# A graph network on one core: how the two attention layers end, where their biases are added, and 16-bit step tables

## What is computed

```
h = relu(layernorm(x)); for i in 0..2: h = in_norm * segment_sum((h * out_norm)[src], dst) @ W[i] + b[i]; relu but for the last
x1 = x + h
h = relu(layernorm(x1))
h1 = relu(gat_conv(h, W1, att1) + b1)
out = x1 + gat_conv(h1, W2, att2) + b2
gat_conv: h = x @ W; softmax over each node's incoming edges and itself of leaky_relu(a_src[src] + a_dst[dst]); weighted sum of h[src]
```

## Time and profile before

| | |
|---|---|
| median of 3 runs | 6783.42 us (6779.98 to 6793.79) |
| span of the profiled execution | 5649.0 us |
| difference between the two, outside the span | 1134.4 us |
| convolution 2, first to last gather | 2259.7 to 3237.3 us |
| attention 0, first to last gather | 3314.8 to 4361.8 us |
| attention 1, first to last gather | 4478.0 to 5527.6 us |
| `rs` of attention 1 there | 5563.0 us |

### The profile page before, as it was taken

How to read it: one execution, slowest core, us unless ns; L and a number is a source line. 1 busy time by engine, 2 the same in 40 slices (tenths; PEclk the granted TensorE clock), 3 DMA queues, 4 the chain that set the end, 5 groups by cost and what they waited for, 6 DMA issues and landing times.

```text
span 5649.0 us, 84292 instructions
## 1 busy us (share of the span) xinstructions
PE 4218.4 (75%) x14997; PEld 2470.4 (44%) x14997; DVE 3705.7 (66%) x12168; ACT 2101.0 (37%) x7038; POOL 4159.4 (74%) x4290
## 2 busy tenths in 40 slices
PE   8677777777777778677777777777777677777772
PEld 7433333343333335333333355555554455555551
DVE  7555555555555554555555568777777677777777
ACT  4000000020000003000000088888887688888881
POOL 8677777777777777777777747777776677777776
PEclk7777677787777668777777778878888888888886
DMA  2443333333333333433333354444444344444444
GB/s 94 117 111 106 106 105 106 105 108 106 106 105 105 105 106 100 131 105 105 106 106 106 106 167 110 110 110 110 110 111 125 99 110 110 110 110 110 110 112 151
DMA packets 309459, 625.61 MB, mean 111 GB/s; under 512 B 85044, under 2 KB 180264, under 8 KB 308937
## 3 DMA queue, kind: packets, MB, share of 16 engines
q0 software_dynamic: 192928, 530.18, 33.3%
q1 hardware_dynamic: 109656, 88.65, 5.0%
q10 hardware_dynamic: 6384, 1.39, 0.1%
HBM read 573.37 MB, written 47.33 MB: 110 GB/s over the span
## 4 chain that ended last, share of the span: by engine, by line
PE 40%; POOL 20%; DMA 14%; issue 11%; DVE 10%; ACT 5%; POOLq 0%; DVEq 0%; SPq 0%; ACTq 0%
PE main L1071 20%; POOL ring L667 13%; PE main L1174 11%; DMA ring<-conv_tab,csrc 9%; DMA ring<-attn_tab,sidx 5%; POOL ring L679 5%; DVE acc L1365 3%; PE main L990 3%; POOL ring L699 2%; PE pso L1094 2%; ACT ring L912 2%; DVE ring L1226 1%; ACT oh L890 1%; DVE ad L1584 1%; PE pso L982 1%
## 5 line engine op out<-in xcount | busy, mean ns | idle before, releaser
L667 POOL DMA_INDIRECT ring<-conv_tab,csrc x2346 | 2222.6, 947 | 749.2 <-issue 590.4
L1071 PE MATMUL main<-ring,oh 128*128 x4992 | 2207.0, 565 | 758.2 <-DVE acc L1365 325.1
L1365 DVE TENSOR_TENSOR acc<-acc,main 128x264 f32 (+2 forms) x4160 | 1761.8, 424 | 1254.2 <-PE main L1071 1157.6
L679 POOL DMA_INDIRECT ring<-attn_tab,sidx x1664 | 1590.8, 956 | 604.5 <-issue 361.7
L1071 PEld LDWEIGHTS main<-ring,oh 128*128 128x128 f32 x4992 | 1092.0, 259 | 1869.7 <-issue 1801.3
L1174 PE MATMUL main<-ring,oh 128*128 128x264 f32 x3328 | 1246.2, 491 | 120.6 <-ACT ring L912 69.2
L912 ACT ACTIVATE ring<-ring 128x64 f32<-128x64 f32 x3328 | 910.9, 343 | 0.0
L1357 DVE TENSOR_SCALAR oh<-iota,dloc 128x128 f32<-128x128 f32 x2505 | 814.8, 325 | 91.9 <-issue 79.6
L1174 PEld LDWEIGHTS main<-ring,oh 128*128 128x128 f32 x3328 | 619.3, 229 | 290.3 <-DVE ring L1690 222.8
L890 ACT ACTIVATE oh<-iota,dloc 128x128 f32<-128x128 f32 x1664 | 528.9, 394 | 3.4 <-DMA attn_tab<-oh 3.4
L1690 DVE TENSOR_TENSOR ring<-ring 128x128 f32<-128x128 f32 x1664 | 463.1, 284 | 0.0
(11 more groups left out here) (212 smaller groups left out, 2993.3 us busy)
## 6 DMA issues: line engine op xcount, KB each, us to landing
ring<-conv_tab,csrc POOLq DMA_INDIRECT x2346, 2.7
ring<-attn_tab,sidx POOLq DMA_INDIRECT x1664
ring<-attn_tab SPq DMA_DIRECT2D x14, 896.0 KB, 8.5
conv_tab<-oh SPq DMA_DIRECT2D x12, 896.0 KB, 4.0
flag_room<-start_rows SPq DMA_DIRECT2D x416, 8.0 KB
flag_room<-end_rows SPq DMA_DIRECT2D x416, 8.0 KB
x_tab<-acc SPq DMA_DIRECT2D x7, 896.0 KB
oh<-x_tab SPq DMA_DIRECT2D x7, 896.0 KB
```

The source lines that it names most:

```text
L667: pool.indirect_dma_start(ring3[:, c % U, 0:C], None, conv_tab[k], bass.IndirectOffsetOnAxis(ap=csrc[:, c:c + 1], axis=0)).then_inc(gather ...
L679: pool.indirect_dma_start(ring3[:, j, 0:TW], None, attn_tab[l], bass.IndirectOffsetOnAxis(ap=sidx[:, i * GB * G + j:i * GB * G + j + 1], a ...
L1071: nc.tensor.matmul(main[s % 4][:, 0:width], oh[:, (s % OHR) * P:(s % OHR + 1) * P], ring[:, bass.ds(slots[s % 8], width)], start=True, sto ...
L1365: nc.vector.tensor_tensor(a, a, main[k][:, 0:width], ALU.add).then_inc(added, 1)
```

## The change

- **Own rows by three engines.** Of each block's 7 tiles, DVE weights the first 4 and POOL the last 3 in attention 0; in attention 1 DVE weights 2, ACT 2 (four instructions of 64 columns a tile) and POOL 3.
- **Cuts.** The first block is done as 2 and 5 tiles, the last as 5 and 2.
- **b1** is added and rectified by ACT at the turned copies, where a feature is a partition: two instructions of 128 columns from `pso` to `aT` in place of one copy. PE turns the tiles from `acc` itself. L1521 and L862 are gone.
- **b2** is subtracted from the stored x1 (whose sign is turned, so that it is added at the end): by POOL on tiles 0 to 41, each once ACT has rectified it, and by DVE on tiles 42 to 48 in one instruction after the last `take_tv` of attention 0. SP's stores of x1 wait for that and stand one block later. L1521 is gone from the end of attention 1 too.
- **The last block of the result** is stored in two pieces, as its parts are done.
- **The step table** holds 16-bit values. The number of loads and of values in each is the same.
- Two loads move: b2 comes with the weights before convolution 1, and b1 a second time, one value a partition.

The diff, cut (the removed lines of `rectify_last` and `normalise` stand in the kernel above as well):

```diff
-        step_words = dram("step_words", (4, SX), I32)
+        step_words = dram("step_words", (4, SX), U16)
...
+        b1T = sb("b1T", [P, 2])
...
-        step_tab = flag_room[H * G:H * G + 4, 0:SX].bitcast(I32)
+        step_tab = flag_room[H * G:H * G + 4, 0:SX // 2].bitcast(U16)
...
+        x1_last_biased = summed
+        POOL_X1 = NT - TB
...
+        def cuts(i):
+            a, b = i * TB, (i + 1) * TB
+            return ((a, a + LAST), (a + LAST, b)) if i == 0 else pieces(i)
+        def own_share(l, i):
+            a, b = i * TB, (i + 1) * TB
+            first, mid = (a + 4, a + 4) if l == 0 else (a + 2, a + 4)
+            return first, mid, b
...
-                    load_bias(b1.rearrange("(o c) -> o c", o=1))
+                    load_bias(b2.rearrange("(o c) -> o c", o=1))
+                    with nc.allow_non_contiguous_dma(reason="one bias value a partition"):
+                        sp.dma_start(b1T[:, :], b1.rearrange("(b p) -> p b", p=P)).then_inc(bias_in, 16)
...
+                def store_x1(i):
+                    if (i + 1) * TB <= POOL_X1:
+                        sp.wait_ge(x1_biased, (i + 1) * TB)
+                    else:
+                        sp.wait_ge(x1_last_biased, NT + 1)
+                    sp.dma_start(rows_of(x1_tab, i, C), acc3[:, i * TB:(i + 1) * TB, 0:C]).then_inc(stored, 16)
                 for i in range(0, NI):
                     store_stage(attn_tab[l], TW, HOPS + l, i)
-                    if l == 0:
-                        sp.wait_ge(mid_ready, i * TB + TB)
-                        sp.dma_start(rows_of(x1_tab, i, C), acc3[:, i * TB:(i + 1) * TB, 0:C]).then_inc(stored, 16)
-                if l:
-                    sp.wait_ge(mid_ready, (l + 1) * NT)
-                    load_bias(b2.rearrange("(o c) -> o c", o=1))
+                    if l == 0 and i:
+                        store_x1(i - 1)
+                if l == 0:
+                    store_x1(NI - 1)
...
-            for q in range(NI - XB, NI):
+            for q in range(NI - XB, NI - 1):
                 store_result(q)
+            a, b = pieces(NI - 1)[0]
+            sp.wait_ge(mid_ready, 2 * NT + b)
+            sp.dma_start(out[a * P:b * P, :].rearrange("(t p) c -> p t c", p=P), acc3[:, a:b, 0:C]).then_inc(stored, 16)
+            sp.wait_ge(mid_ready, 3 * NT)
+            sp.dma_start(out[b * P:NFULL * P, :].rearrange("(t p) c -> p t c", p=P), acc3[:, b:NFULL, 0:C]
+                         ).then_inc(stored, 16)
             sp.dma_start(out[NFULL * P:N, :], acc3[0:NREST, NFULL, 0:C]).then_inc(stored, 16)
-            sp.wait_ge(stored, 16 * (2 * NI + 1))
+            sp.wait_ge(stored, 16 * (2 * NI + 2))
...
+            pool.wait_ge(bias_in, 48)
+            for t in range(POOL_X1):
+                pool.wait_ge(nb_ready, (HOPS - 1) * NT + t + 1)
+                pool.nop(nofuse=True)
+                nc.gpsimd.tensor_tensor(acc[:, t * AW:t * AW + C], acc[:, t * AW:t * AW + C], bias[:, :], ALU.subtract
+                                        ).then_inc(x1_biased, 1)
             for l in range(LAYERS):
                 gather_attn(l)
 
                 pool.wait_ge(nself, EC + l + 1)
                 for i in range(0, NI):
                     pool.wait_ge(row_block_in[i], 16 * (l + 3))
-                    for j in range(TB):
+                    for j in range(own_share(l, i)[1] - i * TB, TB):
...
-            def rectify_last():
-                def one(t):
-                    if t % TB == 0:
-                        act.wait_ge(mid_ready, NT + t + TB)
-                    nb_free(4, t)
-                    nc.scalar.activation(nb_of(t), sums_of(t), ACT.Relu).then_inc(nb_ready, 1)
-                one(0)
-                one(1)
-                copy_rows_T(4, 0)
+            def project_last():
+                def rectify_rows_T(t):
+                    act.wait_ge(rows_T, 4 * NT + t + 1)
+                    past(act, projected, 4 * NT + t - 1)
+                    for b in range(2):
+                        cp = nc.scalar.activation(aT[:, (t % 2) * C + b * P:(t % 2) * C + (b + 1) * P],
+                                                  pso[t % 2][:, b * P:(b + 1) * P], ACT.Relu, bias=b1T[:, b:b + 1])
+                    cp.then_inc(rows_T_copied, 1)
+                act.wait_ge(bias_in, 48)
+                rectify_rows_T(0)
                 for t in range(NT):
-                    if t + 2 < NT:
-                        one(t + 2)
                     if t + 1 < NT:
-                        copy_rows_T(4, t + 1)
+                        rectify_rows_T(t + 1)
                     evacuate(4, t, PW, 1.0)
+            def weigh_own_rows(l):
+                act.wait_ge(nself, EC + l + 1)
+                for i in range(NI):
+                    a, b, _ = own_share(l, i)
+                    act.wait_ge(row_block_in[i], 16 * (l + 3))
+                    for t in range(a, b):
+                        for h in range(H):
+                            r = ring[:, t * C + h * CH:t * C + (h + 1) * CH]
+                            nc.scalar.activation(r, r, ACT.Copy, scale=es[:, t * H + h:t * H + h + 1]
+                                                 ).then_inc(own_weighted, 1)
...
+                if m == HOPS + 1:
+                    for a, b in cuts(t // TB):
+                        if a == t:
+                            pe.wait_ge(mid_ready, NT + b)
...
+                    if m == HOPS + 1:
+                        rows = acc[:, t * AW + b * P:t * AW + (b + 1) * P]
...
+            def bias_last_x1():
+                dve.wait_ge(bias_in, 48)
+                dve.wait_ge(nb_ready, HOPS * NT)
+                a = acc3[:, POOL_X1:NT, 0:C]
+                nc.vector.tensor_tensor(a, a, bias[:, :].rearrange("p (o c) -> p o c", o=1).to_broadcast([P, TB, C]),
+                                        ALU.subtract).then_inc(x1_last_biased, 1)
             def normalise(l):
-                base = chain[0]
-                chain[0] += 2 * NI
-                def part(i, p):
-                    a = acc[:, bass.ds(i * TB * AW, TB * AW)].rearrange("p (t w) -> p t w", w=AW)[:, :, 0:C]
-                    if p == 0:
-                        dve.wait_ge(self_ready, l * NT + i * TB + TB)
-                        own = ring[:, bass.ds(i * TB * C, TB * C)].rearrange("p (t c) -> p t c", c=C)
-                        nc.vector.tensor_tensor(a, a, own, ALU.add).then_inc(dve_chain, 1)
-                    if p == 1:
-                        dve.wait_ge(dve_chain, i * 2 + (base + 1))
-                        a4 = a.rearrange("p t (h c) -> p t h c", h=H)
-                        r4 = rs[:, bass.ds(i * TB * H, TB * H)].rearrange("p (t h o) -> p t h o", h=H, o=1)
-                        nc.vector.tensor_tensor(a4, a4, r4.to_broadcast([P, TB, H, CH]), ALU.mult
-                                                ).then_inc(dve_chain, 1)
-                    if p == 2:
-                        dve.wait_ge(dve_chain, i * 2 + (base + 2))
-                        nc.vector.tensor_tensor(a, a, bias[:, :].rearrange("p (o c) -> p o c", o=1)
-                                                .to_broadcast([P, TB, C]), ALU.add).then_inc(mid_ready, TB)
-                return part
+                def rows(a, b):
+                    return acc[:, a * AW:b * AW].rearrange("p (t w) -> p t w", w=AW)[:, :, 0:C]
+                def by_head(to, factors, a, b):
+                    f4 = factors[:, a * H:b * H].rearrange("p (t h o) -> p t h o", h=H, o=1)
+                    return nc.vector.tensor_tensor(to, to, f4.to_broadcast([P, b - a, H, CH]), ALU.mult)
+                def block(i):
+                    first, mid, _ = own_share(l, i)
+                    dve.wait_ge(row_block_in[i], 16 * (l + 3))
+                    for a, b in cuts(i):
+                        if a < first:
+                            own = ring[:, a * C:min(b, first) * C].rearrange("p (t h c) -> p t h c", h=H, c=CH)
+                            link(by_head(own, es, a, min(b, first)))
+                        if first < min(b, mid):
+                            dve.wait_ge(own_weighted, i * (mid - first) * H + (min(b, mid) - first) * H)
+                        if b > mid:
+                            share = (i + 1) * TB - mid
+                            dve.wait_ge(self_ready, (l * NI + i) * share + b - mid)
+                        own = ring[:, a * C:b * C].rearrange("p (t c) -> p t c", c=C)
+                        link(nc.vector.tensor_tensor(rows(a, b), rows(a, b), own, ALU.add))
+                        last = by_head(rows(a, b).rearrange("p t (h c) -> p t h c", h=H), rs, a, b)
+                        if l < LAYERS - 1:
+                            last.then_inc(mid_ready, b - a)
+                        else:
+                            link(last)
+                            if a == i * TB:
+                                dve.wait_ge(x1_back[i % XB], X1_FROM + 16 * (i // XB + 1))
```

(40 more changed lines are left out.)

22 lines of the change are left out of this document (10 added, 12 removed).

## The result

The changed kernel takes 6874.13 us (median of 4 runs, 6863.84 to 6878.98) against 6782.56 before (4 runs), a ratio of 1.0129 with a 95% interval of 1.0115 to 1.0144: 91 us slower. I had forecast 38 us less.

The account below looks back on a forecast made before the run. POOL's gathers were taken to bound the long stages, leaving only stretches between them. 13.4 + 23.0 + 2.8 + 1.0 - 2.0 = 38.2 us off 6783.4 gave 6745.2 us, 0.56% less; range 6733 to 6764.

Parts of the forecast that it names:

- What bounds the kernel: Long stages: POOL's gathers bound at 1.251 us each in convolution 2; only stretches between gathers count.
- the 2.7 us a group: Attention: DVE's wait for gathered rows, read as spare time per group of 16 gathers, hiding added work.
- 1134.4 us more than the span; I leave that part as it is: Whole kernel: median 6783.4 exceeds the span of 5649.0; the excess was kept unchanged in the forecast time.
- 16-bit tables: Step-table loads: unchanged if priced by values, half if by bytes; 1 us less taken, 0 to 2 in all.
- The slower rival: Attention: narrow 16-value loads above 3.8 us make DVE the pace of 104 groups; at 5 us, 6870; chance 0.04.
- Four times a measured load for half the bytes: Argument against the slower case: the dear narrow load it needs in attention was held unlikely.
- end of attention 0: From `rs` to the next gather: earlier first turn 6.9 us, no PE waiting 6.5, together 13.4 us less; range 9 to 15.
- end of attention 1 and last store: End of attention 1: DVE done 23.0 us earlier, bounds 19 to 29; last store 2.8 us less, 2 to 3.5.
- first end: Attention 0's start: POOL's added b2 subtraction may hold up DVE; 2 us more taken, from nothing to 6.
- the 6 us that the prediction made of the rule: Attention 0's start: a whole POOL instruction once a block, 4 us, plus 2 at the start, as upper loss.

Follow-up runs that it names:

- first run: Kernel before with 32-bit tables, PE's loaded arrival counts kept at 0 or more, on a quick chip: 5660.83 us against 5660.94 of before, ratio 0.9999.
- third: Changed kernel with 32-bit tables and clamped arrival counts, on a quick chip: 5626.4 us, ratio 0.9937 to before.
- sixth: Kernel before with 32-bit tables and clamped arrival counts, on a slow chip: 6793.03 us (one run), beside 6789.17 of before.
- thirteenth: Changed kernel with 32-bit tables and clamped arrival counts, on a slow chip: 6750.53 us against 6789.38 of before, ratio 0.9939.
- the ends alone in the third set: Changed kernel with 32-bit tables and clamped arrival counts, measured again on another quick chip: 5615.44 us, ratio 0.9930 to before.

## Why the prediction was wrong

**What bounds the kernel** held for the chip of the profile and not for that of the times. POOL bounds the long stages at 1.25 us a gather on the quick chips. On the slow ones the steps are late, the gathers stand 1.455 us apart waiting for them, and the 2.7 us a group of the earlier trace rows don't exist: PE is a whole ring behind, and DVE never waits for gathered rows. The step that failed is "1134.4 us more than the span; I leave that part as it is". It was no part outside the span: on both kinds of chip the span is some 2 us under its own execution's time. The profiled execution was of another kind than the timed ones, and every cover read from it was in doubt.

**16-bit tables** is the term of the sum that failed: 1 us less was forecast, "nothing changes, or half". Measured are 3.2 to 3.4 times the 32-bit price on every chip, and some +5 us on a quick chip (2.6 behind each attention, one load of 16 values: 3.79 - 1.10 = 2.7) or +120 on a slow one. The register loads of before could not tell values from bytes, and I took the two readings for the bounds, though a type that no row showed had no bound from above. By the Trainium skill (DMA: Bandwidth & Descriptors, latency and other measured facts) a `tensor_load` has a floor of some 600 ns. The 0.59 us of 8 32-bit values agree with that, the 1.92 us of 8 16-bit ones say that it is no guide to the price of a load.

**The slower rival** had the right edit and, by chance, nearly the right size (6870 us), with 0.04 for it. Its mechanism was another: DVE as the pace of the 104 groups, at a load of more than 3.8 us. DVE's load of 16 takes 3.59, and on a quick chip that leaves a fifth of the wait for rows (284.6 us to 57.9), so POOL stays the pace. On a slow one there is no such wait to use up, and the loss is mainly the drained backlog, 91 of 129 us. "Four times a measured load for half the bytes" was no argument against it.

**The ends** came out as forecast, on either kind of chip. Quick: first run against third; slow: sixth against thirteenth, which are two chips. Each entry is from one execution; the two traces of the changed kernel on slow chips differ by up to 2 us in a gap.

| term | forecast | quick | slow |
|---|---|---|---|
| end of attention 0 | -13.4 | 116.6 to 103.7: -12.9 | 144.9 to 130.5: -14.4 |
| end of attention 1 and last store | -23.0 - 2.8 | 122.6 to 95.7: -26.9 | 151.0 to 124.7: -26.3 |
| first end | +2 | 77.6 to 79.9: +2.3 | 114.8 to 113.3: -1.5 |
| all, by the times | -37.2 | -34.5 and -38.6 | -38.9 |

The steps behind them, from the ends alone in the third set: `rs`, the first and the last turn of the end of attention 0 and the next gather (answering to the earlier trace rows),
```profile
4402.99 1.38 DVE L1843 RECIPROCAL rs<-rs 128x196 f32<-128x196 f32 x1
```
```profile
4407.23 1.08 PE L1038 MATMUL pso<-ident,acc 128*128 128x128 f32 x4 [6.87 <-issue]
```
```profile
4465.33 0.38 PE L1038 MATMUL pso<-ident,acc 128*128 128x128 f32 x2
```
```profile
4471.20 0.99 POOL L707 DMA_INDIRECT ring<-attn_tab,sidx  x1 [27.65 <-DMA attn_tab<-oh]
```
The first turn comes 2.9 us after `rs` (forecast 3 to 4), the next gather 66.8 us after it (67). The clock stayed at 0.50, 1.2 GHz, until 4416.4, 9.2 us after PE took up work and not 5.7 as in the earlier trace rows; the last turn came 61.0 us after `rs` for 60.4 in the sum, and the gather 5.9 behind it where it had been 6.7. Windows of that stretch, columns as in the earlier trace rows:
```profile
4412.00:4416.40 4.40, 4.40 (x13) 3.36 (x14) 4.26 (x3) 1.64 (x5) 4.40 (x4) 0.50 0.00 0
4416.40:4467.00 50.60, 50.60 (x273) 42.33 (x272) 31.98 (x24) 41.35 (x136) 27.15 (x13) 1.00 0.33 112
```
PE is busy without a gap from 4412 on, as the sum wanted. At the end of attention 1 (answering to the earlier trace rows), two blocks, DVE's last instruction and the last store:
```profile
5566.78 2.32 DVE L1597 TENSOR_TENSOR acc<-acc,ring 128x1792 f32<-128x1792 f32 x1
...
5574.85 2.32 DVE L1597 TENSOR_TENSOR acc<-acc,ring 128x1792 f32<-128x1792 f32 x1
...
5611.29 0.69 DVE L1606 TENSOR_TENSOR acc<-acc,oh 128x512 f32<-128x512 f32 x1
```
```profile
5612.40 0.29 SPq L619 DMA_DIRECT2D out_dram<-acc  x1
```
8.07 us a block (forecast 8.1); 55.5 us from `rs` to DVE's last (56.2); the span's end at 5616.8, 4.8 us behind (4.0).

The first end cost +2.3 and +1.8 us on quick chips (77.6 to 79.9 and 79.4) and nothing that can be seen on a slow one (114.8 to 113.3 on two chips; 139.9 both with the tables alone and with the whole change, on one), near what I took from the earlier trace rows. By the rule of the Trainium skill that was weighed against it (SBUF — State Buffer, the practical consequences) a DVE instruction with two SBUF inputs contends with a GpSimd instruction that reads SBUF, and the later one is blocked. Here the trace of the ends alone agrees with it for single instructions:
```profile
3260.15 0.73 POOL L722 TENSOR_TENSOR acc<-acc,bias 128x256 f32<-128x256 f32 x1 [0.61 <-ACT nb L873]
```
```profile
3260.16 0.99 DVE L1515 SCALAR_TENSOR_TENSOR acc<-acc,inorm,oh 128x256 f32<-128x256 f32 x1
```
Before it took 0.45 us. All 49 of them lost 4.5 us together, while the statistics (L1522), with one input, stay at 0.42 each. What failed is the 6 us that the prediction made of the rule: it put a whole POOL instruction on the chain in every block, and of the 4.5 us the stage shows 2.3. The pair of the earlier trace rows, with another POOL instruction, doesn't show the block; why is open.

So 120 - 39 = 81 us is the change on a slow chip, by its two parts measured alone, on two chips; the whole was measured at +73.5 and +91.6. On a quick chip it is +5 - 38 = -33, measured -33.5.

**A version that beats both** is the change without its tables: 5615 and 6751 us, where before takes 5654 and 6789 beside it, and the changed kernel 5621 and 6863 to 6874.

## What to carry to other kernels

Compare the span of a profile with the time of the runs before anything else; a gap of a fifth was no overhead here but another kind of execution, whose covers must not be used. Don't bound the price of an operand type from rows of another type. Work that is hidden behind a bounding engine still shows where the stage ends, as often as the hidden engine is steps behind: read from the trace how many products start behind the last gather (8 or 64 steps here) before calling it free.

## What the runs showed of the hardware

- A register load of 8 values from SBUF takes 0.59 us as int32 and 1.92 as uint16 on PE (0.60 and 1.83 on DVE); of 16 values 1.10 and 3.79 (1.10 and 3.59).
- Halving the bytes of a gathered row (1024 to 512) left the gather's 1.25 us as they were.
- Two chips of four ran the same program 20% slower. In the convolutions there some 850 instructions of PE's sequencer took 0.7 us and not 0.04 or 0.05, and a group of 8 steps took 11.8 us while gathers ran and 5.5 behind them. Neither halved bytes nor fewer such instructions brought the pace back.
- A DVE instruction with two SBUF inputs took 0.99 us and not 0.45 when it started beside a POOL instruction over two SBUF inputs; one with a single input kept its 0.42.
